# Edge counts built without the staging engine, and four small stages after them joined into one

## The chip, the cores and the metric

The kernel runs on one core of one Trainium2 chip. The metric is the time of one execution on the device, in microseconds (us), lower is better. The kernel before took 2728.32 us (median of 3 runs, 2724.99 to 2728.71).

## The reference, cut to what matters

A graph network of four layers over 2500 nodes with 256 features and 80000 edges. Each layer adds a message-passing part and a routed feed-forward part to x:

```python
edge_index = stack([src, dst])                       # dst is sorted; low numbers are the most frequent
x = x + L0_gnn(_layernorm(x), edge_index, ...)       # mean of x[src] over the edges of each dst, two linear maps
x = x + L0_ffn(_layernorm(x), ...)                   # experts
x = x + L1_gnn(...); x = x + L1_ffn(...)             # normalised by degree, then experts
x = x + L2_gnn(...); x = x + L2_ffn(...)
x = x + L3_gnn(...); x = x + L3_ffn(...)             # attention over edges, then experts
```

Every message-passing part needs only how often each pair (src, dst) occurs, and the degrees (how many edges end at a node). The kernel therefore first turns the edge list into a dense matrix of counts, and uses it four times.

## The kernel before

The program is a row of phases, each with its own block of per-engine instruction streams. At a phase's end all engines meet at a barrier. The change touches the first five: `phase_setup`, `phase_counts`, `phase_degrees`, `phase_transpose_weights` and the first `phase_norm` ("n0"). The sixth is the first gather ("g0"), where the message passing of layer 0 starts. Its first instruction is ScalarE's `g_y` at L847.

**Setup** (L90 to L236) loads the edges as 125 groups of 640, computes two numbers for each edge on VectorE (DVE), `lo` (src modulo 128) and `key` (which encodes dst and src's tile), turns them with TensorE (PE) so that a column holds 128 edges (625 columns in all), and copies them to `lo_col` and `key_col`. Then it finds, for each strip of 16 dst nodes, the first and last column that has an edge of it (`m.ranges`, 160 strips), and the number of units (`m.units`), where a unit is 4 columns.

**Counts** (L239 to L447). There are 20 tiles of 8 strips. For a strip, each unit of 4 columns goes through a ring of SR = 4 slots:

- GpSimd (POOL) loads the tile's 16 bounds into registers (L266), and for each unit writes the unit's 8 edge columns, less the strip's offset, into `key_stage` (L284).
- DVE, in one flat loop over all units (L300), waits for `staged` and `slot_free`, and builds two one-hot matrices: `hot_lo` (4 x 128 wide) and `hot_key` (4 x 320 wide), both from L295.
- PE loads the 16 bounds itself once for each tile (L266), and for each strip opens a PSUM bank with a matmul of zeros (L317), loops over the units with 4 matmuls each (L319, L324), closes with a two-column matmul that tells `summed` (L329), and then takes away the high part of the strip before (L335, `rest`). In strips 2 to 6 of a tile it also turns a fifth of the tile before (L345, 8 matmuls for high and low).
- ScalarE (ACT) copies high (L376) and low (L381) of each strip, and of each fifth the turned high rows (L389) and low rows (L390), each with a sum into `deg_part`.
- SyncE (SP) stores four pieces of 640 KB for each tile (L432, L434, L437, L439). At the end it waits for all of them before the phase may end.

**Degrees** (L580 to L638): DVE sums `deg_part`, takes roots and reciprocals, and the inverse root degrees are spread to a row by 5 f32 matmuls (L637) and 5 copies of ACT.

**Weights and spare row** (L641 to L739): three weight matrices are loaded and turned on PE (L703), and nodes with a degree over 2048 get a spare row: flags, a running sum, `spare_pick` (f32, 128 x 2560, L730), 20 f32 matmuls (40 passes in the profile, L709), an indirect load by POOL (L687), a multiplication (L739), and a store (L672).

**Norm n0** (L504 to L574): DVE takes the statistics of 20 tiles of x, a root on ACT, the normalised tiles (L518), and PE turns them (40 transposes, L574) with 10 copies of ACT (L560).

## Time and profile before

| what | us |
|---|---|
| median of 3 runs | 2728.32 |
| the profiled execution's own time | 2723.45 |
| its span in the trace | 2721.7 |
| setup, until the counts' barrier | 0 to 36.7 |
| counts, until PE's last strip is summed | 36.7 to 409.5 |
| last rows and stores | 409.5 to 425.4 |
| degrees, weights and spare row | 425.4 to 461.6 |
| norm n0 | 461.6 to 480.3 |
| everything from g0 on | 480.3 to 2721.7 |

Times in the trace are from the start of the span. The lines of the source are given as L and a number. "q" behind an engine means its sequencer, which computes registers, branches and waits while the engine's datapath may be busy or idle. "idle before <-X" says for how long the engine stood and who released it; "issue" means that the profile shows nobody that it waited for.

### The profile page before, as it was taken

What the parts mean: (1) busy time and instruction counts of PE and PEld (TensorE: products, weight loads), DVE (VectorE), ACT (ScalarE), POOL (GpSimd) and SP (SyncE); (2) the same over time, 40 slices, a digit from 0 to 9 for tenths busy, and PEclk for the clock granted to TensorE, in tenths of its full rate; (3) what the DMA queues carried; (4) which work ended last, traced back from release to release, by engine and by line L of the source; (5) the groups of instructions that cost most, each with busy time, mean ns of one, the idle gap of its engine ahead of it and who ended that gap; (6) DMA issues with size and microseconds to landing.
All of it is one profiled execution on the core that took longest, in us unless ns stands there. A gap on an engine that the chain in (4) does not pass through costs nothing. (4 is left out here: it accounts for less than half of the span.)

```text
span 2721.7 us, 43328 instructions
## 1 busy us (share of the span) xinstructions
PE 2017.2 (74%) x12867; PEld 1606.2 (59%) x12868; DVE 1540.7 (57%) x2761; ACT 1134.4 (42%) x2295; POOL 512.8 (19%) x581
## 2 busy tenths in 40 slices
PE   3778884893592953882979559934899995699998
PEld 1445553453591532881349449932888885488887
DVE  7877664216347035665124555556899996355554
ACT  0347882101443012782034337712434431276765
POOL 3332320000401001671000057713000000010110
PEclk8999996995795986896989759966999997599999
DMA  1123442410102302563510135521222220000001
GB/s 47 59 116 154 193 193 84 157 39 1 32 1 79 121 5 91 162 184 104 192 33 1 61 127 173 166 92 57 66 84 84 93 86 12 14 13 23 12 24 38
DMA packets 133356, 222.53 MB, mean 82 GB/s; under 512 B 17565, under 2 KB 98973, under 8 KB 133075
## 3 DMA queue, kind: packets, MB, share of 16 engines
q1 hardware_dynamic: 122119, 190.51, 20.7%
q0 software_dynamic: 11088, 30.03, 3.7%
q8 instruction: 93, 1.52, 0.2%
q14 instruction: 56, 0.46, 0.1%
HBM read 146.27 MB, written 74.24 MB: 81 GB/s over the span
## 5 line engine op out<-in xcount | busy, mean ns | idle before, releaser
L807 PE MATMUL g_ps<-g_at,g_y 128*128 128x512 f16 x1170 | 261.8, 386 | 122.1 <-DMA g_at<-counts_t_high 116.5
L1927 DVE TENSOR_TENSOR e_h_low<-x_feat,e_h_high 128x512 fp32r<-128x512 f32 (+1 forms) x240 | 169.6, 709 | 244.7 <-ACT e_h_high L1852 244.7
L2213 DVE SCALAR_TENSOR_TENSOR att_masked<-dinv_row,att_thr,x_feat 128x512 fp32r<-128x512 f32 x400 | 277.2, 747 | 31.4 <-PE att_ps L2324 23.3
L807 PEld LDWEIGHTS g_ps<-g_at,g_y 128*128 128x128 f16 x1170 | 115.6, 99 | 265.5 <-DMA g_at<-counts_t_high 117.1
L1851 ACT ACTIVATE x_feat<-e_hps,e_b 128x512 f32<-128x512 f32 (+1 forms) x240 | 177.7, 740 | 202.0 <-issue 99.4
L2324 PE MATMUL att_ps<-att_xl_parts,att_masked 128*128 128x260 f32 x1600 | 229.9, 294 | 25.7 <-DVE att_masked L2213 23.4
L2324 PEld LDWEIGHTS att_ps<-att_xl_parts,att_masked 128*128 128x128 f32 x1600 | 203.0, 189 | 51.5 <-DVE att_masked L2213 40.4
L324 PE MATMUL count_ps<-hot_key,hot_lo 128*128 x960 | 195.8, 325 | 35.2 <-DVE hot_key L295 23.5
L295 DVE TENSOR_TENSOR hot_key<-o_tok,key_stage 128x1280 f16 x240 | 196.8, 820 | 0.0
L1794 PE MATMUL e_yps<-e_w_high,e_h_high 128*128 128x256 f32 (+1 forms) x640 | 182.2, 285 | 2.2 <-DVE e_h_low L1927 2.2
L1794 PE MATMUL e_yps<-e_w_high,e_h_low 128*128 128x256 f32 (+1 forms) x640 | 180.9, 283 | 0.0
L1794 PE MATMUL e_yps<-e_w_low,e_h_high 128*128 128x256 f32 (+1 forms) x640 | 180.9, 283 | 0.0
L1852 ACT ACTIVATE e_h_high<-e_hps,e_b 128x512 fp32r<-128x512 f32 (+1 forms) x240 | 176.5, 735 | 0.0
L284 POOL TENSOR_TENSOR key_stage<-dinv_row,o_tok x240 | 121.9, 508 | 268.0 <-issue 176.8
L1766 PE MATMUL e_hps<-e_x_high,e_w_high 128*128 128x512 f32 (+1 forms) x320 | 126.5, 395 | 60.0 <-POOL e_w_low L1720 45.9
L324 PEld LDWEIGHTS count_ps<-hot_key,hot_lo 128*128 x960 | 95.7, 100 | 120.1 <-issue 70.9
L1720 POOL TENSOR_TENSOR e_w_low<-a3xn_tok,e_w_high 128x512 fp32r<-128x512 f32 x23 | 30.1, 1336 | 710.2 <-ACT e_w_high L1858 710.2
L295 DVE TENSOR_TENSOR hot_lo<-o_tok,key_stage 128x512 f16 x240 | 102.1, 425 | 92.9 <-PE count_ps L324 61.8
L1457 POOL DMA_INDIRECT e_x_rows<-xn_rows,e_get_i x104 | 129.0, 1241 | 59.2 <-issue 29.9
L376 ACT ACTIVATE turn_high<-count_ps 128x320 f16<-128x320 f32 x160 | 74.8, 468 | 147.8 <-PE count_ps L329 147.7
L2324 PE MATMUL att_ps<-att_xl_parts,att_plain 128*128 128x260 f32 x800 | 107.8, 294 | 32.5 <-ACT att_plain L2293 32.5
L2293 ACT ACTIVATE att_plain<-x_feat 128x512 fp32r<-128x512 f16 x200 | 107.4, 620 | 49.0 <-PE att_ps L2324 42.5
(466 smaller groups left out, 4981.8 us busy)
## 6 DMA issues: line engine op xcount, KB each, us to landing
g_at<-counts_t_high SPq DMA_DIRECT2D x12, 2560.0 KB
x_feat<-counts_high SPq DMA_DIRECT2D x40, 640.0 KB, 4.1
e_w_in<-in_L_ffn_W SPq DMA_DIRECT2D x35, 512.0 KB, 4.0
e_w_in<-in_L_ffn_expert_w SPq DMA_DIRECT2D x56, 256.0 KB, 3.8
counts_t_high<-turn_high SPq DMA_DIRECT2D x20, 640.0 KB, 3.4
counts_t_low<-turn_low SPq DMA_DIRECT2D x20, 640.0 KB, 4.8
counts_high<-row_high SPq DMA_DIRECT2D x20, 640.0 KB, 3.0
counts_low<-row_low SPq DMA_DIRECT2D x20, 640.0 KB, 4.2
```

Of the source, the lines that this page charges most:

```text
L284: pool.tensor_tensor(stage[:, ds(slot_of(n), 1), :, :, :].rearrange("p a i u d -> p (a i) u d"), edge_col[:, :, ds(c, UN)].unsqueeze(3).to ...
L295: return dve.tensor_tensor(out.rearrange("p a u (w d) -> p (a u) w d", d=2), numbers.rearrange("p (w d) -> p w d", d=2).unsqueeze(1).to_br ...
L324: mm = pe.matmul(acc[:, q % 4, 0:KW], hot_lo[:, ds(at, 1), j, :].rearrange("p a l -> p (a l)"), hot_key[:, ds(at, 1), j, :].rearrange("p a ...
L807: pe.matmul(ps[:, k, :], y2[:, part, s, k * P:(k + 1) * P], at[:, b % 2, :, s, :], start=(s == 0 and part == 0), stop=False, skip_group_ch ...
L1457: pool.indirect_dma_start(x_rows[:, b % XB, q, :], None, m.xn_rows[:, :], bass.IndirectOffsetOnAxis(ap=r.get_i[:, b * RT + q:b * RT + q + ...
L1766: mm = pe.matmul(h_ps[0][:, f, 0:width(b)], w_parts[0][w][:, u, k, f * P:(f + 1) * P], x_parts[x][:, k, b * BLK:b * BLK + width(b)], start ...
L1794: mm = pe.matmul(y_ps[0:tokens, q, 0:D], h_parts[-1][h][:, v % 2, k, q * P:q * P + tokens], w_parts[-1][w][:, u, k, :], start=(k == 0 and ...
L1851: act.activation(h_sb[i][:, f, 0:w], h_ps[i][:, f, 0:w], func, bias=bias, scale=scale)
L1852: act.activation(h_parts[i][0][:, v % 2, f, 0:w], h_ps[i][:, f, 0:w], func, bias=bias, scale=scale).then_inc(h_act[i], 1)
L1927: dve.tensor_tensor(h_parts[i][1][:, v % 2, f, 0:w], h_sb[i][:, f, 0:w], h_parts[i][0][:, v % 2, f, 0:w].bitcast(F32), ALU.subtract).then_ ...
L2213: dve.scalar_tensor_tensor(S[:, n % RING, :], EL[:, it % 2, u - 1, :], thr[:, t, h:h + 1], A[:, t, :], ALU.is_gt, ALU.mult).then_inc(maske ...
L2324: mm = pe.matmul(ps[:, n % 2 * TB + q, 0:PW], side[:, q * P:(q + 1) * P], moving, start=(t == 0), stop=(t == NT - 1))
```

## The change

Three functions become part of others, and two are rewritten.

- **Setup.** The two numbers of an edge now carry its strip: `lo` = 128 x (strip within a lot of 32) + lane - 2048, and `key` = 320 x lot + 16 x tile + place - 2048. They are stored as f16, each twice, in `m.edge_col`, by two copies of ACT. The column ranges come from dst alone, ahead of the two numbers. Units are kept for each strip (`m.strip_units`), and their sum is gone. ACT runs one Sqrt at the start.
- **Counts.** POOL has no part. DVE loops over lots, strips and units with register bounds (32 registers loaded for each 16 strips), compares the edge columns directly with a slice of `m.numbers` that depends on the strip and the lot, and computes slot and count in registers. The ring has SR = 8 slots. PE loads 32 unit counts for each 4 tiles. The closing two-column matmul and its semaphore are gone (but for the very first strip): ACT's copy of a strip now waits for `rest` of the strip before it. The two row copies become one of 128 x 1024 with one sum.
- **Norm n0's first part** (statistics, root, normalised tiles) stands behind the last one-hots in the counts phase. ACT takes the root after the last `copy_low`, ahead of the last five row copies.
- **One stage, `prepare`**, does degrees, weights, spare row and the turning of x. The wait for all stores moves into its SP stream; only POOL's indirect load waits for that. `spare_pick` and its matmuls are f16.

```diff
-SR = 4
+SR = 8
+GT = 4
+LOT = 32
...
-            with pool.Fori(0, NT) as t:
-                bounds(pool, t, regs)
...
-            with dve.Fori(0, units) as n:
-                at = slot_of(n)
-                column = stage[:, ds(at, 1), :, :, :].rearrange("p a i u d -> p (a i) u d")
-                dve.wait_ge(staged, n + 1)
-                dve.wait_ge(slot_free, n + 1)
-                one_hot(hot_lo[:, ds(at, 1), :, :], lo_no, P, column[:, 0, :, :])
-                one_hot(hot_key[:, ds(at, 1), :, :], m.src_no[:, 0:KW], KW, column[:, 1, :, :]).then_inc(built, 1)
+            def next_unit(eng, need, at, inside):
+                eng.reg_add(at, at, KW)
+                eng.reg_alu(inside, at, (SR - 1) * KW, ALU.is_le)
+                eng.reg_alu(at, at, inside, ALU.mult)
+                eng.reg_add(need, need, 1)
...
+                with dve.Fori(0, NS // LOT) as h:
+                    first_key = dve.snap(h * KW, min_val=0, max_val=NS // LOT * KW - KW)
+                    for i in range(LOT // (2 * QS)):
+                        dve.reg_load(regs, m.ranges[0:1, ds(h * (LOT // (2 * QS)) + i, 1), :].rearrange("a t n -> a (t n)"))
+                        for q in range(2 * QS):
+                            lanes = (i * 2 * QS + q) * P
+                            dve.reg_mov(column, regs[q])
+                            with dve.Fori(regs[q], regs[2 * QS + q], UN):
+                                dve.wait_ge(slot_free, need)
+                                c = dve.snap(column, min_val=0, max_val=NCOL)
+                                slot = dve.snap(at, min_val=0, max_val=(SR - 1) * KW)
+                                one_hot(hot_lo[:, :, ds(slot, P)], m.numbers[:, lanes:lanes + P], P, m.edge_col[:, 0, ds(c, UN), :])
+                                one_hot(hot_key[:, :, ds(slot, KW)], m.numbers[:, ds(first_key, KW)], KW,
+                                        m.edge_col[:, 1, ds(c, UN), :]).then_inc(built, 1)
+                                dve.reg_add(column, column, UN)
+                                next_unit(dve, need, at, inside)
...
+                    with pe.Fori(0, regs[i * QS + q]):
+                        pe.wait_ge(built, need)
+                        slot = pe.snap(at, min_val=0, max_val=(SR - 1) * KW)
+                        for j in range(UN):
+                            mm = pe.matmul(acc[:, q % 4, 0:KW], hot_lo[:, j, ds(slot, P)], hot_key[:, j, ds(slot, KW)],
+                                           start=False, stop=False, skip_group_check=True)
+                        mm.then_inc(slot_free, 1)
+                        next_unit(pe, need, at, inside)
-                pe.matmul(acc[:, q % 4, 0:2], m.zeros16[:, :], m.src_no[:, 0:2], start=False, stop=False,
-                          skip_group_check=True).then_inc(summed, 1)
...
+                def group(g, first):
+                    pe.reg_load(regs, m.strip_units[0:1, ds(g * (GT * QS), GT * QS)])
+                    for i in range(GT):
+                        tile(g * GT + i, i % 2, i, not first or i > 0)
...
-                act.activation(row_high[:, u, cut], tps[:, (u + b) % 2, 0, :], ACT.Copy, accum_out=m.deg_part[:, ds(t, 1), b])
-                act.activation(row_low[:, u, cut], tps[:, (u + b) % 2, 1, :], ACT.Copy,
-                               accum_out=m.deg_part[:, ds(t, 1), NB4 + b]).then_inc(row_out, 1)
+                    act.activation(row[:, u, :, cut], tps[:, (u + b) % 2, :, :], ACT.Copy,
+                                   accum_out=m.deg_part[:, ds(t, 1), b]).then_inc(row_out, 1)
...
+                for t in range(NT):
+                    own.step(dve.bn_stats(x_st[:, t, :], m.x[:, t, :]))
+                dve.wait_ge(x_own, NT)
+                stats_steps(own, dve, x_st, mean, var, tmp, False)
+                dve.sem_inc(want_root, 1)
+                dve.wait_ge(root, 1)
+                own.join(dve.reciprocal(tmp, var))
+                for t in range(NT):
+                    dve.tensor_scalar(m.xn[:, t, :], m.x[:, t, :], x_stat[:, 0, t:t + 1], x_stat[:, 2, t:t + 1], ALU.subtract, ALU.mult)
...
-            for u in range(2):
-                sp.wait_ge(high_stored[u], NT // 2 * 16)
-                sp.wait_ge(low_stored[u], NT // 2 * 16)
-                sp.wait_ge(row_stored[u], NT // 2 * 32)
+        prepare(nc, m, mats, all_stored)
```

In `prepare` the streams are in this order. PE: 4 of the 10 blocks of turned x, the two flag matmuls, the other 6 blocks, the turned maximum, the 20 pick matmuls, the 12 weight transposes, the 5 spreading matmuls. DVE: degrees, flags, the running sum, `pick`, the reciprocals, the index of the spare row, the 20 diagonal blocks, the maximum, and the product of the fetched row. ACT: block 0 of x, the root, blocks 1 to 9, the 3 weights, the 5 spread rows. SP: the three weight loads, the wait for all stores (which releases POOL's indirect load), and the spare row's store.

## Rows read from the trace of the kernel before

**Rows 1.** Windows of the stages: busy us (instructions) of each engine, granted clock, DMA share, GB/s

```profile
36.70:409.50 372.80, 294.95 (x2198) 175.51 (x2198) 276.33 (x480) 224.68 (x693) 121.91 (x240) 0.93 0.33 130
461.60:480.30 18.70, 7.25 (x40) 7.01 (x40) 14.54 (x49) 5.83 (x11) 0.00 (x0) 0.59 0.00 0
480.30:2721.70 2241.40, 1688.97 (x10496) 1404.95 (x10496) 1211.33 (x2134) 890.37 (x1556) 381.47 (x312) 0.86 0.23 74
```

**Rows 2.** Waits of PE in the counts: total us, times, longest

```profile
PE count_ps L317 <- issue: 36.3, 18, 5.4
PE count_ps L324 <- DVE hot_key L295: 23.5, 50, 2.8
```

**Rows 3.** Register loads by source line: ns min/median/max, first and last start

```profile
L266 PEldq TENSOR_LOAD <-ranges x20: 1103/1107/3205, 37.0 to 396.4; - x20
L292 DVEq TENSOR_LOAD <-units x1: 553/553/553, 36.9 to 36.9; - x1
```

**Rows 4.** One of DVE's unit loops, time order: start, busy, engine, line

```profile
43.44 0.43 DVE L295 TENSOR_TENSOR hot_lo<-o_tok,key_stage 128x512 f16 x1
43.80 0.81 DVE L295 TENSOR_TENSOR hot_key<-o_tok,key_stage 128x1280 f16 x1
44.53 0.43 DVE L295 TENSOR_TENSOR hot_lo<-o_tok,key_stage 128x512 f16 x1
```

**Rows 5.** Sequencer instructions by source line (DVE's loop, SP's three register adds)

```profile
L300 DVEq COMPARE_BRANCH  x240: 50/56/75, 40.4 to 404.1; - x120
L295 DVEq FUSED_REGOPS  x480: 93/93/110, 39.9 to 403.9; - x160
L441 SPq FUSED_REGOPS  x20: 60/100/147, 117.1 to 420.8; - x20
```

**Rows 6.** PE in time order, dense strips, then two late strips

```profile
51.22 0.80 PE L324 MATMUL count_ps<-hot_key,hot_lo 128*128 x4 [0.41 <-DVE hot_key L295]
52.44 0.77 PE L324 MATMUL count_ps<-hot_key,hot_lo 128*128 x4 [0.41 <-DVE hot_key L295]
...
358.36 0.17 PE L329 MATMUL count_ps<-o_tok,zeros 128*128 128x2 f16 x1
...
359.64 0.17 PE L329 MATMUL count_ps<-o_tok,zeros 128*128 128x2 f16 x1
```

**Rows 7.** Window of one late tile

```profile
357.19:370.73 13.54, 11.15 (x96) 7.13 (x97) 9.31 (x16) 11.84 (x39) 4.06 (x8) 1.00 0.48 194
```

**Rows 8.** ACT, one row pair in time order, then a copy of 1024 by source line

```profile
206.60 0.60 ACT L389 ACTIVATE row_high<-cturn_ps 128x512 f16<-128x512 f32 x1
...
207.19 0.59 ACT L390 ACTIVATE row_low<-cturn_ps 128x512 f16<-128x512 f32 x1
...
L854 ACT ACTIVATE g_self<-x_feat x1: 1040/1040/1040, 485.1 to 485.1; 128x1024 f32<-128x1024 f32 x1
```

**Rows 9.** Setup on DVE, its end, and the first one-hot, time order

```profile
10.24 0.49 DVE L163 TENSOR_SCALAR edge_b<-edge_i 125x640 int32<-125x640 int32 x1 [9.15 <-DMA edge_i<-in_dst]
...
15.75 0.82 DVE L176 TENSOR_REDUCE key_ends<-edge_f 125x5 f32<-125x640 f32 x1
...
20.55 0.79 DVE L188 COPY bounds_row<-turn_ps 80x625 f32<-80x625 f32 x1
...
35.66 0.14 DVE L217 CAST units<-ends_row 1x1 int32<-1x1 f32 x1
...
40.09 0.43 DVE L295 TENSOR_TENSOR hot_lo<-o_tok,key_stage 128x512 f16 x1 [4.29 <-POOL key_stage L284]
```

**Rows 10.** From the last strip to g0, time order

```profile
409.47 0.17 PE L329 MATMUL count_ps<-o_tok,zeros 128*128 128x2 f16 x1
...
425.48 0.36 DVE L598 TENSOR_REDUCE deg<-deg_part 128x20 f32<-128x200 f32 x1 [20.47 <-PEq L2451]
...
446.03 5.43 PE L709 MATMUL spare_ps<-spare_rows,spare_pick 128*128 128x2 f32 x40
...
456.97 0.89 DVE L739 TENSOR_SCALAR spare_low<-spare_low,spare_at 128x2560 f16<-128x2560 f16 x1 [5.13 <-DMA spare_low<-counts_low,spare_at_i]
...
461.60 6.63 DVE L504 BATCH_NORM_STATS2 n_st<-x_tok 128x6 f32<-128x256 f32 x20 [3.74 <-PEq L2451]
...
480.31 1.06 ACT L847 ACTIVATE g_y<-xn_tok 128x1024 f16<-128x1024 f32 x1 [0.78 <-PEq L2451]
```

More of the change, by code:

```diff
@@ L173, in _ @@
-            own.join(dve.scalar_tensor_tensor(t_dst, key, -float(NT - 1), t_dst, ALU.mult, ALU.add))
-            own.join(dve.scalar_tensor_tensor(key, t_src, float(WD) / P, t_dst, ALU.mult, ALU.add))
-            by_column = key.rearrange("p (k e) -> p k e", k=GC)
+            dst_f, key_f = edge_t[0:NG, 0, :], edge_t[0:NG, 1, :]
+            lot, lane, tile, place, group = (edge_b[0:NG, i, :] for i in range(5))
+            own.join(dve.tensor_copy(dst_f, dst_i))
+            by_column = dst_f.rearrange("p (k e) -> p k e", k=GC)
@@ L182, in _ @@
-            for i, col in enumerate((m.lo_col, m.key_col)):
-                own.step(dve.tensor_copy(col[:, 0:NCOL].rearrange("p (g k) -> p k g", k=GC),
-                                         ps[:, 2 * i:2 * i + 2, :, :].rearrange("p b q n -> p (b q) n")[:, 0:GC, 0:NG]))
+            own.step(dve.tensor_scalar(lot, dst_i, (LOT - 1) * WD, (P // WD).bit_length() - 1, ALU.bitwise_and, ALU.logical_shift_left))
+            own.step(dve.tensor_scalar(lane, src_i, P - 1, None, ALU.bitwise_and))
+            own.step(dve.tensor_scalar(tile, src_i, (P // WD).bit_length() - 1, -WD, ALU.logical_shift_right, ALU.bitwise_and))
@@ new lines, in _ @@
+            own.step(dve.tensor_scalar(place, dst_i, WD - 1, None, ALU.bitwise_and))
+            own.join(dve.tensor_scalar(group, dst_i, (LOT * WD).bit_length() - 1, None, ALU.logical_shift_right))
+            own.step(dve.scalar_tensor_tensor(edge_f[0:NG, 0, :], lot, float(LOW), lane, ALU.add, ALU.add))
+            own.join(dve.scalar_tensor_tensor(key_f, group, float(KW), tile, ALU.mult, ALU.add))
+            own.step(dve.scalar_tensor_tensor(edge_f[0:NG, 1, :], place, float(LOW), key_f, ALU.add, ALU.add))
@@ L213, in _ @@
             own.join(dve.tensor_copy(span_i[0:1, :], span))
-            own.join(dve.tensor_scalar(span_i[0:1, :], span_i[0:1, :], UN.bit_length() - 1, None, ALU.arith_shift_right))
-            own.join(dve.tensor_copy(span, span_i[0:1, :]))
-            own.join(dve.tensor_reduce(ends_row[0:1, 1, 0:1], span, AX.X, ALU.add))
-            own.join(dve.tensor_copy(m.units[0:1, :], ends_row[0:1, 1, 0:1]))
+            own.join(dve.tensor_scalar(m.strip_units[0:1, :], span_i[0:1, :], UN.bit_length() - 1, None, ALU.arith_shift_right))
+        @block.scalar
+        def _(act):
+            act.wait_ge(made, 1)
+            act.activation(m.spare_col[:, 0:1], m.ones[:, 0:1], ACT.Sqrt)
+            act.wait_ge(turned, 2 * GC)
+            for i in range(2):
+                act.activation(m.edge_col[:, i, 0:NCOL, :].rearrange("p (g k) d -> p k g d", k=GC),
+                               ps[:, 2 * i:2 * i + 2, :, :].rearrange("p b q n -> p (b q) n")[:, 0:GC, 0:NG].unsqueeze(3)
+                               .to_broadcast([P, GC, NG, 2]), ACT.Copy)
         @block.tensor
@@ L221, in _ @@
             pe.wait_ge(made, 3)
-            pe.wait_ge(dve_own, 10)
+            pe.wait_ge(dve_own, 4)
+            for i in range(2):
+                for k in range(GC):
+                    pe.transpose(ps[0:NH, 4 + 2 * i + k // 4, k % 4, 0:NG], bounds[0:NG, i, k, :],
+                                 m.ident[0:NG, 0:NG]).then_inc(turned_rng, 1)
+            pe.wait_ge(dve_own, 12)
             for i in range(2):
```

689 lines of the change are left out of this document (335 added, 354 removed).

## The prediction

> **What bounds the kernel now.** I read the windows by stage first. What the change touches ends at 480.3 us; the 2241.4 us behind it [rows 1] run the same instructions on the same data, so I carry them over unchanged. The counts are the long stage, 372.8 us, and no engine is full in it: PE 294.95, DVE 276.33, ACT 224.68, POOL 121.91 [rows 1]. Next the order in time. DVE alone would make a unit in 1.09 us (43.44 to 44.53) [rows 4], PE takes 1.22 us for each further unit of a strip (51.22 to 52.44, of which 0.41 us stands between the matmuls) and 1.28 us for a late strip of one unit (358.36 to 359.64) [rows 6]. 240 units at 1.09 are 262 us, so DVE has slack, and PE with its sequencer sets the pace. Third the waits: PE stands 36.3 us ahead of L317, at 18 tile starts [rows 2], and these are the register loads of 16 bounds, 20 of them, 1.1 us each and up to 3.2 [rows 3]. A late tile takes 13.54 us, of which ACT is busy 11.84 [rows 7]: ACT is right behind PE. After the last strip (409.47) the phases stand in a row, each behind a barrier, until g0 starts at 480.31: 70.8 us [rows 10], with short dependent instructions that leave every engine mostly idle.
>
> **Part 1, setup.** The range work starts at 20.55 us, behind seven elementwise steps on each edge's two numbers, and setup ends at 35.8 [rows 9]. Now a cast (0.49, as its neighbour there), two reductions (0.82 each) and a copy (0.6) come first, from 10.24 to 13.0; then five integer steps, 0.4 apart, to 15.0, and three of two tensors at 0.8, to 17.4 in place of 20.55. The three last steps (the sum of the units) save 0.85. So setup ends 4.0 us earlier. From setup's end to the first one-hot it is 4.3 us now (35.8 to 40.09), through POOL's load and staging [rows 9]. DVE will instead load 32 registers itself: 1 took 0.55, 16 take 1.11 [rows 3], so 0.037 each, 32 take 1.7; with barrier and loop entry 3.5 us. Saved 4.8 in all; bounds 3 and 6. The two copies and the extra table load on ACT are over before the ranges are, 15 us of cover.
>
> **Part 2, counts.** Four terms.
> (a) Loads. PE's 19 loads inside the stage become 4, of 32 registers. Low end 1.7 (above), high end 3.2 + 16 x 0.037 = 3.8. I take 2.8, which makes 11 us in place of 36.3: -25. The other load is DVE's, 10 of them; 8 slots at 1.3 us are 10 us of cover, so nothing, and at most 9 x 1.7 = 15 if DVE has no lead.
> (b) ACT. The second copy of a row pair starts 0.59 us behind the first (206.60 to 207.19), so a pair takes 1.18; a copy lasts 0.01 longer than that step, and one of 1024 lasts 1.04, so it takes 1.03. That is 0.15 off five times a tile, so ACT falls from 11.84 to 11.1 a tile [rows 7, 8]. With its mean load wait of 1.1 gone a late tile would fall to 12.4; ACT at 11.1 is late next, and in the strips with row copies (about 0.7 for high and low, plus 1.03, against PE's 1.28) it sets the pace until the strips without let it catch up. I give back 0.25 us for each of 12 late tiles: +3.
> (c) Register work. The new loops add up to five register operations for each unit on PE and on DVE, and take away PE's and DVE's mask and add. One fused instruction did three adds on SP in 0.06 to 0.10 us [rows 5]. PE's sequencer is exposed between matmuls in 80 further units and 60 strips without turning: 140 x 0.05 = +7. Bounds: 0 and 240 x 0.15 = 36.
> (d) The closing matmul goes, 0.03 us apart from its neighbour: nothing. That ACT's copy now waits for `rest` costs nothing where ACT is late anyway, and at most 0.1 x 160 = 16 where not; it is inside (c)'s upper bound. POOL's staging goes; it released DVE but rarely, so nothing.
> Sum of part 2: -25 + 3 + 7 = -15. DVE must keep up: 240 units in about 350 us is 1.46 us a unit, against 1.09 now. Its loop holds six sequencer instructions, among them two fused ones of 0.093 and the branch of 0.056 [rows 5]. I put the new unit at 1.2 to 1.3.
>
> **Part 3, the tail.** From the last strip to g0 is 70.8 us now. New, from the last strip X:
> - rest, high, low as before: X + 3, then the root, and five row copies at 1.1 to 1.3 as PE's turnings feed them: X + 10. DVE is some units ahead of PE, so statistics (6.63, and 1.3 of small steps) are done by then, and the 20 normalised tiles (6.55 for all now, by the same instruction) end at X + 10 to X + 13. With the barrier `prepare` starts at X + 12.5. The landing of the last stores, now 5 us ahead of 425.48 [rows 10], is only waited for by the indirect load.
> - In `prepare`, T after its start: 16 transposes of x (7.25 us for 40 [rows 1], so 2.9), flags and matmuls 3.7; running sum 6.3; `pick` as f16, twice the 0.82 of a one-hot of 1280, 7.9. PE finishes the 40 transposes at 8.3, the maximum, then 20 pick matmuls: now 40 passes in 5.43 [rows 10], as f16 half the passes, 2.0 to 2.7, so 10.9. Index at 11.2, indirect load 5.1 as now: 16.3. PE meanwhile turns the weights (3.0, as now) to 13.9, and spreads the row in about 5.6: 19.5. DVE's last diagonal block waits for the fourth of those: 18.5, then the maximum and the product (0.89): 19.9. From there to the next phase is 3.74 us after 457.86 now, by the store's landing: 23.6.
> So g0 starts at X + 36.1 in place of X + 70.8: -34.7. The four pieces that go from the path: the statistics and the normalising (9.9 under the counts' tail), the turning of x (under the flags and the sum), one barrier and a store's landing, and the f32 pick. Bounds: -25 (the spreading, the indirect load and the store each 3 us late) and -40 (the indirect load hidden, DVE's work ended by X + 10).
>
> One rule of the Trainium skill speaks against part 2. The trace shows 16 registers in 1.11 us as the median of PE's 20 loads, and 3.2 at most [rows 3]. "Runtime: NRT & Kernel Launch", section "Instruction fetch mechanics", puts a TENSOR_LOAD at about 200 ns for each register even in bulk. By that rule 32 registers take 6.4 us, and PE's four loads would cost 26 and not 11 us: the sum would be 15 us higher. The median load here contradicts it, the slowest fits it.
>
> **Sum.** -4.8 - 15 - 34.7 = -54.5. The profiled execution took 2723.45 (its span is 2721.7, 1.75 outside), which gives 2669; the median of the runs lies 4.9 above it: 2728.3 - 54.5 = 2673.8. I say 2673. A difference of under 0.2% (5.5 us) can't be told from none here.
>
> **Rivals.**
> - *DVE becomes the pace* (20%). For: up to five register operations, three run-time addresses and a nested loop in its sequencer, which takes part of each 1.09 us now. Against: fused operations are cheap [rows 5]. At 1.5 us a unit the counts take 240 x 1.5 + 17 of loads = 377 against 369.4 (40.09 to 409.47) [rows 9, 10]: +8, with the normalising behind it 3 later: -4.8 + 8 - 32 = -29, 2699.
> - *Slower than before, by the same sequencer* (5%). It decides from (369.4 + 4.8 + 32 - 17) / 240 = 1.62 us a unit. At 1.7 the counts take 425, and the whole is +19: 2747. It would need 0.5 us more of sequencer work for each unit than the loop now has in all its instructions' own durations.
> - *Loads of 32 registers are slow* (10%), 6.4 us each, as if the slow rows were the rule (3.2 for 16): 4 x 6.4 = 26, so part 2 gives nothing and the sum is -39.5: 2689.
> - *All of the loads' time comes back* (15%): PE's loads hide in its queue, register work costs nothing, ACT catches up: part 2 is -30 to -36, and the sum -70 to -75: 2655.
> - *`prepare` is longer* (7%): its spare-row chain stands behind PE's transposes and the spread rows; at 33 us and not 23.6 the tail gives -25: 2683.
> - The forecast itself has 43%.
>
> **How the numbers follow.** The range 2642 to 2702 holds the forecast, the slow loads, the longer stage, most of the full gain, and DVE's pace up to 1.5. Faster by over 0.2% is all but the second rival and a part of the first: 0.93; same 0.02; slower 0.05.
>
> **What would show it.** In the profile after: the first one-hot near 35.3 us; one-hots that start less than 1.3 us apart in the dense strips with PE's 1.2 to 1.3 us between them; register loads of PE at 4 inner places, 1.7 to 3.8 us; a late tile of about 12.4 us with ACT busy 11; the last strip near 390; the gap from it to L847's successor near 36 us. Wrong would be: DVE's one-hots with gaps not ended by PE (its sequencer is the pace); a span from the last strip to g0 over 45 us; or any change behind g0, which I hold at 2241 us.

## The result

The kernel after takes 2627.15 us (median of 4 runs, 2624.22 to 2630.38), beside 2728.45 for the kernel before in the same comparison: a ratio of 0.9632, 95% interval 0.9615 to 0.9649. It is 101 us faster. The forecast was 2673 us, 55 us faster, in a range from 2642 to 2702; the measured time lies 15 us below the range. The direction was right, the size was not.

The profiled execution took 2628.58 us and has a span of 2626.9. First the windows of its stages (window, length, then busy us and instructions of PE, PE's weight loads, DVE, ACT and POOL, granted clock, DMA share, GB/s):

```profile
35.30:350.00 314.70, 264.94 (x2040) 161.43 (x2040) 269.82 (x507) 208.88 (x506) 0.00 (x0) 0.98 0.37 155
348.65:380.46 31.81, 20.19 (x131) 14.00 (x129) 18.16 (x72) 18.56 (x39) 2.20 (x7) 0.77 0.49 179
380.46:2626.90 2246.44, 1691.19 (x10496) 1407.77 (x10496) 1211.54 (x2134) 890.69 (x1556) 381.91 (x312) 0.86 0.23 73
```

Against [rows 1] and [rows 10], with the counts taken from the first one-hot to the start of the last unit's last matmul:

| stretch | before | after | measured | forecast |
|---|---|---|---|---|
| start to the first one-hot | 40.09 | 35.59 | -4.5 | -4.8 |
| counts | 369.2 | 313.0 | -56.2 | -15 |
| tail, from there to g0 | 71.1 | 31.8 | -39.3 | -34.7 |
| g0 to the end | 2241.4 | 2246.4 | +5.0 | 0 |
| sum | 2721.7 | 2626.9 | -94.8 (rounded terms -95.0) | -54.5 |

The stretch behind g0 runs the same instructions; over the seventeen changed kernels here it lies between 2240.1 and 2248.3 us, and the kernel before, at 2241.4, lies inside that spread, so nothing shows the +5.0 to be an effect of the change. Almost the whole miss is in the counts. Their waits (total us, times, longest):

```profile
DVE hot_lo L478 <- PE count_ps L526: 31.4, 33, 4.3
PE count_ps L520 <- issue: 18.9, 5, 5.7
PE count_ps L526 <- DVE hot_key L478: 13.6, 37, 1.2
```

The load waits of PE that [rows 2] has at 18 tile starts, 36.3 us, are now 18.9 us at 5. The loads themselves (count, ns min/median/max, first and last start):

```profile
L563 PEldq TENSOR_LOAD <-strip_units x5: 2331/2566/4297, 32.9 to 300.5; - x5
L486 DVEq TENSOR_LOAD <-ranges x10: 2112/2933/5872, 32.9 to 315.7; - x10
```

Loads give back 17 to 18 us of the 56 (PE's waits fall by 17.4, its loads from 32.3 us in all to 14.4). DVE's ten loads, which I had put at nothing, took 31.7 us in all, but PE's waits for `hot_key` did not grow: 13.6 us in all, against 23.5 [rows 2].

PE's granted clock moved too, and I had not priced that. Over the counts it is 0.94 before and 0.98 after. At the lower of its two levels (1.2 GHz) two matmuls of a unit start 0.26 us apart, otherwise 0.14 to 0.15; 120 of the 960 unit matmuls ran so before, 43 after. 18 of them stand at the start of the counts in both. The others come in short stretches, eleven before and three after, and each begins 1 to 5 us after the start of a load for which PE stood (before: loads at 90.8, 117.0 and 141.9, lower level from 94.7, 118.6 and 145.9). That is worth at most some 9 us of the 56 (77 x 0.12, an estimate that puts every one of them on the path), and runs 8 and 11 below speak for less.

The rest is in the pace. A dense strip is one with many units, as in the first tiles; a late strip has one. In a dense strip DVE and PE now go in step (start, busy, and in brackets the idle time before it and who ended it); first DVE, then PE:

```profile
50.59 0.41 DVE L478 TENSOR_TENSOR hot_lo<-o_tok,dinv_row 128x512 f16 x1
50.93 0.81 DVE L478 TENSOR_TENSOR hot_key<-o_tok,dinv_row  x1
51.66 0.41 DVE L478 TENSOR_TENSOR hot_lo<-o_tok,dinv_row 128x512 f16 x1
...
52.73 0.41 DVE L478 TENSOR_TENSOR hot_lo<-o_tok,dinv_row 128x512 f16 x1
```

```profile
50.83 0.74 PE L526 MATMUL count_ps<-hot_key,hot_lo 128*128 x4
51.90 0.72 PE L526 MATMUL count_ps<-hot_key,hot_lo 128*128 x4 [0.33 <-DVE hot_key L478]
52.97 0.76 PE L526 MATMUL count_ps<-hot_key,hot_lo 128*128 x4 [0.36 <-DVE hot_key L478]
```

A unit takes 1.07 us on both. Before, PE took 1.22 [rows 6] and DVE could do 1.09 [rows 4]. A late tile went from 13.54 us [rows 7] to 11.40, with ACT busy 10.59, and its row copy of 1024 lets the next copy start 1.00 us later (233.89 to 234.89):

```profile
229.12:240.52 11.40, 10.09 (x89) 6.59 (x89) 9.30 (x17) 10.59 (x28) 0.00 (x0) 1.00 0.56 230
```

```profile
233.89 1.03 ACT L594 ACTIVATE count_row<-cturn_ps 128x1024 f16<-128x1024 f32 x1
234.80 0.21 ACT L594 ACTIVATION_READ_ACCUMULATOR count_row<-cturn_ps  x1
234.89 0.45 ACT L581 ACTIVATE turn_high<-count_ps 128x320 f16<-128x320 f32 x1
```

The tail, in time order, to be read against [rows 10]: PE, then DVE, then ACT's first instruction of g0.

```profile
359.45 3.52 PE L325 MATMUL turned_ps<-ident,xn_tok 128*128 128x128 f32 x16 [2.51 <-PEq L457]
367.56 0.64 PE L348 MATMUL spare_ps<-spare_rows,spare_pick 128*128 128x4 f16 x20 [1.46 <-DVE spare_pick L390]
370.32 6.15 PE L332 MATMUL deg_ps<-deg_diag,ones 128*128 128x512 f32 x10
```

```profile
365.92 1.49 DVE L390 TENSOR_TENSOR spare_pick<-spare_no,spare_col 128x2560 f16<-128x2560 f16 x1
...
375.69 0.89 DVE L412 TENSOR_SCALAR spare_low<-spare_low,spare_at 128x2560 f16<-128x2560 f16 x1
```

```profile
380.46 4.84 ACT L877 ACTIVATE g_y<-xn_tok 128x1024 f16<-128x1024 f32 x5 [3.36 <-PEq L2477]
```

### The profile page after: what moved, and what is told of

Its sections match the earlier page's. It is cut to its first block and busy times, and to the rows that moved or that the text cites. A ratio compares the mean times of both kernels' runs of the same rounds, so it can differ in the third digit from the quotient of the medians.

```text
span 2626.9 us, 39157 instructions
## 1 busy us (share of the span) xinstructions
PE 1981.1 (75%) x12688; PEld 1587.2 (60%) x12689; DVE 1519.6 (58%) x2752; ACT 1120.7 (43%) x2100; POOL 392.4 (15%) x339
## 5 line engine op out<-in xcount | busy, mean ns | idle before, releaser
L2243 DVE SCALAR_TENSOR_TENSOR att_masked<-dinv_row,att_thr,x_feat 128x512 fp32r<-128x512 f32 x400 | 277.2, 747 | 31.8 <-PE att_ps L2354 23.6
L478 DVE TENSOR_TENSOR hot_key<-o_tok,dinv_row x240 | 195.4, 814 | 0.0
L526 PE MATMUL count_ps<-hot_key,hot_lo 128*128 x960 | 177.1, 309 | 18.5 <-DVE hot_key L478 13.6
L2323 ACT ACTIVATE att_plain<-x_feat 128x512 fp32r<-128x512 f16 x200 | 107.5, 620 | 49.3 <-PE att_ps L2354 42.8
L1824 PEld LDWEIGHTS e_yps<-e_w_high,e_h_high 128*128 128x128 f32 (+1 forms) x640 | 121.2, 189 | 8.5 <-issue 3.7
L2354 PEld LDWEIGHTS att_ps<-att_xl_parts,att_plain 128*128 128x128 f32 x800 | 105.2, 193 | 34.6 <-ACT att_plain L2323 34.6
L1796 PE MATMUL e_hps<-e_x_low,e_w_high 128*128 128x512 f32 (+1 forms) x320 | 126.0, 394 | 0.0
```

Of the source, the lines that this page charges most:

```text
L478: return dve.tensor_tensor(out.rearrange("p u (w d) -> p u w d", d=2), numbers.rearrange("p (w d) -> p w d", d=2).unsqueeze(1).to_broadcas ...
L526: mm = pe.matmul(acc[:, q % 4, 0:KW], hot_lo[:, j, ds(slot, P)], hot_key[:, j, ds(slot, KW)], start=False, stop=False, skip_group_check=True)
L1796: mm = pe.matmul(h_ps[0][:, f, 0:width(b)], w_parts[0][w][:, u, k, f * P:(f + 1) * P], x_parts[x][:, k, b * BLK:b * BLK + width(b)], start ...
L1824: mm = pe.matmul(y_ps[0:tokens, q, 0:D], h_parts[-1][h][:, v % 2, k, q * P:q * P + tokens], w_parts[-1][w][:, u, k, :], start=(k == 0 and ...
L2243: dve.scalar_tensor_tensor(S[:, n % RING, :], EL[:, it % 2, u - 1, :], thr[:, t, h:h + 1], A[:, t, :], ALU.is_gt, ALU.mult).then_inc(maske ...
L2323: act.activation(plain[:, n % ARING, :], A[:, t, :], ACT.Copy).then_inc(plain_a, 1)
```

## The experiments

Each kernel is the one after with one edit, unless it says otherwise; the edits are cut to their main lines (`...`). "Measured" gives the median in us, its ratio to the kernel before and the ratio's 95% interval. "Counts" and "tail" are the two stretches of the table, in us, from the profile of that run; after has 313.0 and 31.8. Each comes from one profiled execution. Runs 6 and 14, which leave the counts' loops as they are, have 312.4 and 312.9, and run 7, which only takes DVE's norm out of that phase, 314.3: differences of 1 to 2 us in the counts can't be told from none.

**1. Slot arithmetic on PE.** After, PE keeps byte offset and count in registers, and the four operations of `next_unit` are one fused sequencer instruction of 154 ns. Here PE masks a counter, as before.

```diff
-                        pe.wait_ge(built, need)
-                        slot = pe.snap(at, min_val=0, max_val=(SR - 1) * KW)
+                        n = pe.snap(used)
+                        at = n & (SR - 1)
+                        pe.wait_ge(built, n + 1)
...
-                        next_unit(pe, need, at, inside)
+                        pe.reg_add(used, used, 1)
```

> The changed kernel, with PE's unit loop computing its slot as the kernel before did (a counter, a mask, and a multiplied slot in each matmul's address) and nothing else changed. Theory A (the unit itself became shorter in PE's sequencer, 1.21 to 1.07 us): the pace of PE in strips of two units goes from 2.21 back to about 2.5 us a strip, the counts from the first one-hot to the last sum (313 us) grow by 15 to 30 us. Rival B (the deeper ring freed the engines from each other): no change, under 3 us.

Measured: 2636.59 us, ratio 0.9671 (0.9639 to 0.9704). Counts 325.4, +12.4. The edit undoes PE's half of the term that I had booked at +7, and that half alone is a gain. PE's sequencer, after and with the mask (ns min/median/max):

```profile
L526 PEldq FUSED_REGOPS  x720: 55/55/65, 36.9 to 348.2; - x180
L460 PEldq FUSED_REGOPS  x240: 149/154/168, 37.3 to 348.4; - x120
L524 PEldq FUSED_REGOPS  x240: 59/59/59, 36.8 to 347.8; - x120
```

```profile
L528 PEldq FUSED_REGOPS  x960: 55/55/65, 36.8 to 360.7; - x192
L528 PEldq ALU_OP  x240: 36/36/42, 36.7 to 360.2; - x120
```

After has five fused instructions for a unit beside its branch: three addresses, one that holds the wait and the first address, and the update. With the mask there are seven: four addresses, mask, copy and add. A unit of a dense strip takes 1.09 to 1.14 us in place of 1.07.

**2. Ring of four slots.**

```diff
-SR = 8
+SR = 4
```

> The changed kernel with SR = 4. Theory A: only the register loads lose cover, DVE's ten and PE's four, 0 to 12 us on the counts, and tiles without a load keep their 17.5 and 11.4 us. Rival B (the ring): every tile grows, the counts by 20 us or more.

Measured: 2623.52, 0.9623 (0.959 to 0.9656), counts 312.2. The deeper ring shows no gain.

**3. The closing matmul of a strip.**

```diff
+                    pe.matmul(acc[:, q % 4, 0:2], m.zeros16[:, :], m.numbers[:, 0:2], start=False, stop=False,
+                              skip_group_check=True).then_inc(summed, 1)
...
-                    act.wait_ge(rest_mm, t * QS + (q + 2))
+                    act.wait_ge(rest_mm, t * QS + (q + 1))
```

> The changed kernel with the closing two-column matmul and its semaphore back in each strip; ACT's high copy waits for it again. Theory A: 160 strips at 0.03 to 0.06 us, 5 to 10 us on the counts at most. Rival C (the closing matmul held PE's queue between strips, and its going is most of the 0.43 us by which a strip of two units got shorter): 0.15 us or more for each strip, over 20 us.

Measured: 2628.11, 0.964 (0.9601 to 0.9679), counts 312.4. Nothing, as forecast.

**4. PE's loads, 8 registers for each tile in place of 32 for four.**

```diff
-                    pe.reg_load(regs, m.strip_units[0:1, ds(g * (GT * QS), GT * QS)])
                     for i in range(GT):
+                        pe.reg_load(regs[i * QS:(i + 1) * QS], m.strip_units[0:1, ds(g * (GT * QS) + i * QS, QS)])
```

> The changed kernel with PE loading 8 unit counts at each tile (20 loads) and not 32 for four tiles (5 loads). Theory A (loads cost by the number of them, not of registers): 15 more stalls at 1 to 3 us: the counts grow by 15 to 35 us. Rival D (loads cost by the register, the same 160 registers in all): under 3 us.

Measured: 2620.55, 0.9612 (0.958 to 0.9644). Counts 308.9, 4.1 less than after, although there are four times as many loads:

```profile
L564 PEldq TENSOR_LOAD <-strip_units x20: 588/594/785, 33.2 to 333.8; - x20
```

The cost is by register: 8 take 0.59, 16 take 1.10 [rows 3], 32 take 2.13 in run 8, which is 64 ns for each (0.51 for 8, 1.03 for 16) and some 0.08 fixed. What the change gained is that it loads one count for a strip, not a first and a last column: 160 registers and not 320. Grouping them by four tiles gained nothing; its loads were 14.4 us in all, these 12.1. A late tile with a load of 8 takes 11.64 us here, one without a load took 11.38 after, and one with a load of 32 took 14.48: much of a short load is hidden, little of a long one. The granted clock, too, stays at its full level from 40.0 us on (up to there no clock is recorded, and the ten slow matmuls of this run stand there):

```profile
35.91:344.80 308.89, 264.22 (x2037) 159.04 (x2038) 269.71 (x507) 207.13 (x504) 0.00 (x0) 1.00 0.38 158
```

**5. Two row copies again.**

```diff
-                    act.activation(row[:, u, :, cut], tps[:, (u + b) % 2, :, :], ACT.Copy,
-                                   accum_out=m.deg_part[:, ds(t, 1), b]).then_inc(row_out, 1)
+                    act.activation(row[:, u, 0, cut], tps[:, (u + b) % 2, 0, :], ACT.Copy, accum_out=m.deg_part[:, ds(t, 1), b])
+                    act.activation(row[:, u, 1, cut], tps[:, (u + b) % 2, 1, :], ACT.Copy,
+                                   accum_out=m.deg_part[:, ds(t, 1), NB4 + b]).then_inc(row_out, 1)
```

> The changed kernel with ACT's row copy split in two again, 512 wide each, each with its own sum. If ACT is what sets the late tiles (11.38 us, steps of 1.66 where rows are copied): each of the five steps goes to 1.81, a late tile to about 12.0, the counts grow by 8 to 12 us. If PE's or DVE's sequencer sets them: under 2 us.

Measured: 2631.35, 0.9648 (0.962 to 0.9676). Counts 322.1, +9.1. The late tile is 0.75 us longer, which is five times the 0.15 that the prediction had for a pair: ACT is the pace there, and every saved tenth on it counts.

```profile
231.38:243.53 12.15, 10.12 (x89) 6.61 (x89) 9.24 (x17) 11.35 (x38) 0.00 (x0) 1.00 0.54 216
```

The two copies and the next one on ACT: from 231.25 to 232.39 it is 1.14 us, where one copy of 1024 takes 1.00.

```profile
231.25 0.74 ACT L594 ACTIVATE count_row<-cturn_ps 128x512 f16<-128x512 f32 x1
231.82 0.75 ACT L595 ACTIVATE count_row<-cturn_ps 128x512 f16<-128x512 f32 x1
232.39 0.60 ACT L581 ACTIVATE turn_high<-count_ps 128x320 f16<-128x320 f32 x1
```

**6. All stores waited for at the end of the counts.** Three waits of SP stand there again.

```diff
+                for u in range(2):
+                    sp.wait_ge(high_stored[u], NT // 2 * 16)
+                    sp.wait_ge(low_stored[u], NT // 2 * 16)
+                    sp.wait_ge(row_stored[u], NT // 2 * 32)
```

> The changed kernel with the wait for all stores back at the end of the counts' own block. If the landing of the last stores was on the path: the stretch from the last sum to g0's first instruction (31.6 us) grows by 3 to 5 us. If DVE's normalised tiles end later than the landing anyway: under 1 us.

Measured: 2626.94, 0.9632 (0.9604 to 0.966). In the profile the tail is 35.0, +3.2. The median of the times does not show it, and its interval is too wide to show or exclude 3 us.

**7. The norm behind the counts.** Statistics, root and normalised tiles stand in a block of their own ahead of `prepare`.

```diff
+        with nc.Block() as block:
+            @block.vector
+            def _(dve):
+                own = Steps(dve, x_own)
...
+            @block.scalar
+            def _(act):
+                act.wait_ge(want_root, 1)
+                act.activation(x_stat[:, 1, :], x_stat[:, 1, :], ACT.Sqrt).then_inc(root, 1)
```

> The changed kernel with statistics, root and normalised tiles in a block of their own between the counts and the joined stage. If what was hidden under the end of the counts is what the tail gained: the stretch from the last sum to g0 grows by about 15 us (6.6 + 1.3 + 6.6 + a barrier of 0.8), less the 2 to 4 us by which the counts' block ends earlier without it: 11 to 14. If the joined stage waits for something else: under 5.

Measured: 2641.56, 0.9686 (0.9655 to 0.9716). Tail 47.7, +15.9: the two passes over x, 6.63 and 6.54 us, with the small steps and a barrier, are bare again.

```profile
361.26 6.63 DVE L644 BATCH_NORM_STATS2 x_st<-x_tok 128x6 f32<-128x256 f32 x20 [20.93 <-PEq L457]
...
369.57 6.54 DVE L651 TENSOR_SCALAR xn_tok<-x_tok,x_stat 128x256 f32<-128x256 f32 x20
```

**8. Turnings apart from each other.** If ACT sets the pace in strips with a row copy, they should not stand in a row.

```diff
-TURNS = (2, 3, 4, 5, 6)
+TURNS = (1, 2, 4, 5, 7)
```

> The changed kernel with the five turnings of a tile in strips 1, 2, 4, 5 and 7 in place of 2 to 6. If ACT's row of five 1.66 us steps sets a late tile (11.38 us) while PE and DVE could do with 10: the tile falls to about 10.6, the counts by 8 to 12 us. If the pace of PE's sequencer is the floor: under 2 us.

Measured: 2615.22, 0.9589 (0.9559 to 0.962), counts 304.3, 8.7 less than after. The late tile is 10.96 us with ACT busy 10.71; and PE's loads no longer begin beside the issue of a store, 2.13 to 2.33 us in place of 2.33 to 4.30, which is 3.5 us less in all. The rows are the late tile, then the loads:

```profile
225.05:236.01 10.96, 9.59 (x92) 6.62 (x89) 9.02 (x17) 10.71 (x27) 0.00 (x0) 1.00 0.58 239
```

```profile
L563 PEldq TENSOR_LOAD <-strip_units x5: 2129/2145/2328, 32.9 to 294.1; - x5
```

**9. POOL stages the keys again**, one operation and one semaphore ahead of DVE.

```diff
+                            pool.wait_ge(built, n + 1)
+                            pool.tensor_tensor(stage[:, ds(n & (SR - 1), 1), :, :, :].rearrange("p a i u d -> p (a i) u d"),
+                                               m.edge_col[:, :, ds(c, UN), :], none, ALU.add).then_inc(staged, 1)
...
+                                dve.wait_ge(staged, need)
                                 dve.wait_ge(slot_free, need)
```

> The changed kernel with POOL staging each unit's columns again (a copy, since the strip stays inside the pairs) and DVE reading the stage and waiting for it. If the staging was part of the pace: POOL starts a unit 0.6 us after the ring lets it and loads 32 registers for each 2 tiles at 3 us, so the counts grow by 10 to 20 us, mostly in tiles after a load. If POOL's stage was always ahead (my forecast held it for nothing): the counts grow by under 3 us, and the first one-hot comes 1 us later.

Measured: 2638.05, 0.9674 (0.9653 to 0.9696). First one-hot at 36.35, +0.8, and counts 322.0, +9.0. Tile 0, all dense strips, takes 49.82 in place of 45.49; late tiles are unchanged (11.36). So the cost is in the dense strips: tile 0 and, by 0.2 to 2.4 us each, tiles 1 to 4 have nearly all of it. The edit does not isolate POOL, for DVE's loop gets a second wait, a counter and a mask with it.

**10. Five parts together, then with staging.** Ring of 4, PE's mask, closing matmul, two row copies, and 16 registers loaded for each tile (eight of them are used); the second kernel adds POOL's staging.

```diff
+                        at16 = g * (GT * QS) + (i * QS if first and i == 0 else i * QS - QS)
+                        pe.reg_load(regs[0:2 * QS], m.strip_units[0:1, ds(at16, 2 * QS)])
```

> The changed kernel with ring of 4, PE's slot as before, the closing matmul, two row copies, and PE loading 16 registers at each of 20 tiles as before. Alone the slot gave +12.4 us on the counts, the rows +9.1, ring and closing matmul -0.8 and -0.6. Sum with 16 registers a tile (before: 32.3 us of loads in all against 14.4): about 313 + 20 + 14 = 347. If 347 or less is reached, some 22 us of the 56 are still unnamed (POOL's staging); if 365 to 369, these parts are all of it.

Measured: 2664.7, 0.9772 (0.975 to 0.9794), counts 351.5, +38.5. PE's 20 loads are again of 16 registers, 29.0 us in all (32.3 before):

```profile
L566 PEldq TENSOR_LOAD <-strip_units x20: 1102/1108/2694, 32.7 to 374.1; - x20
```

> The same with POOL's staging as well. If the list is complete: counts of 365 to 370 us, as before the change (369.2), and late tiles of 13.5. If under 355: something else in the change (the strip inside the pairs and DVE's own loop) is worth the rest.

Measured: 2675.13, 0.981 (0.9788 to 0.9833), counts 355.8, +42.8. 13.4 us of the 56.2 were left unexplained.

**11. Loads of 8 and the turnings apart, together.** The edits of 4 and 8.

> The changed kernel with PE loading 8 unit counts at each tile and the turnings in strips 1, 2, 4, 5 and 7. The two alone gave -4.1 and -8.7 us on the counts. If they are independent: 300 us of counts, 2614 us. If the loads only filled gaps that the turnings left: 304.

Measured: 2615.87 (2615.18 to 2617.49), 0.9593 (0.9579 to 0.9607). Counts 305.6. They do not add: with the turnings apart the loads of 32 are already short (10.9 us in all, these 12.1). 16 unit matmuls are slow here, all at the start, where run 8 has 47, and yet the counts are no shorter than in run 8: the clock's share of the time is small.

**12. The layout of the ring.** After, a slot is a stretch of columns inside each of a unit's four rows, so one offset serves both one-hot tiles. Here the slot's index is outermost, as before, and both engines mask a counter.

```diff
-            nc.sbuf_tensor("hot_lo", [P, UN, SR * KW], F16) as hot_lo,
-            nc.sbuf_tensor("hot_key", [P, UN, SR * KW], F16) as hot_key,
+            nc.sbuf_tensor("hot_lo", [P, SR, UN, P], F16) as hot_lo,
+            nc.sbuf_tensor("hot_key", [P, SR, UN, KW], F16) as hot_key,
```

> The one-hot tiles with the ring's index outermost, as before, and the slot worked out of a counter on DVE and PE, as before; all else as after. If the 13.4 us that four_parts_and_stage leaves over are PE's address instructions: these take 74 ns again in place of 55, four for a unit, PE needs 1.21 us between the units of a dense strip in place of 1.07, and the counts last about 25 to 30 us longer than after (313.0), 12 to 18 more than in pe_slot_as_before (325.4): some 2652 us in all. If the layout is nothing and the rest comes from the loop of units on DVE (one loop over all units before, loops inside strips after): as pe_slot_as_before, 2636 us and 55 ns.

Measured: 2647.52, 0.9717 (0.9702 to 0.9732). Counts 337.7, which is 12.3 more than in run 1. First PE's sequencer at the line of the unit's matmuls, then PE in a dense strip:

```profile
L528 PEldq FUSED_REGOPS  x960: 74/74/88, 37.4 to 373.7; - x192
```

```profile
50.83 0.80 PE L528 MATMUL count_ps<-hot_key,hot_lo 128*128 x4 [0.41 <-issue]
52.04 0.76 PE L528 MATMUL count_ps<-hot_key,hot_lo 128*128 x4 [0.41 <-issue]
```

74 ns for an address, and 1.21 us from unit to unit. The 0.41 us stands there as "issue". [Rows 6] have the same 0.41 with DVE's name on it: it was PE's own sequencer then too. In time order the kernel before has the same list there: add (L328), branch (208 ns), copy (L320), mask and address (L324), each some 60 ns behind the one ahead of it, with no wait between them:

```profile
L320 PEldq FUSED_REGOPS  x240: 41/41/46, 38.5 to 408.3; - x120
L324 PEldq FUSED_REGOPS  x960: 74/74/88, 41.4 to 409.0; - x192
L324 PEldq ALU_OP  x240: 36/36/42, 41.3 to 408.4; - x120
L328 PEldq FUSED_REGOPS  x240: 42/42/42, 42.1 to 409.2; - x120
```

**13. All parts back.** `four_parts_and_stage` with that layout.

> four_parts_and_stage with the old slot layout on top: ring of 4, closing matmul, two row copies, 16 registers loaded for each tile, POOL staging the keys, slot from a counter, ring index outermost. Setup, tail and DVE's loops inside the strips stay as after. If nothing else made the counts long: 369 us from the first one-hot to the last sum, as before (369.2), and some 2689 us. If the strips' loops on DVE are worth something by themselves: less, near 356 to 360, and 2675 to 2680 us.

Measured: 2678.16, 0.9826 (0.9811 to 0.9841). Counts 365.5, against 369.2 before: the difference of 56.2 is undone but for 3.7. The second and the third tile have that remainder (3.8 us, of which 1.1 are shorter load stalls); no late tile differs by more than 0.6. The clock came back as well: 111 unit matmuls at the lower level, against 120 before and 43 after.

**14. The pick in 32 bits.**

```diff
-        nc.sbuf_tensor("spare_pick", [P, NT, P], F16) as pick,
+        nc.sbuf_tensor("spare_pick", [P, NT, P], F32) as pick,
```

> After, with the pick of spare rows in 32-bit floats (numbers, rows and pick), as before. If the 16-bit pick is what made the tail shorter than forecast (pick matmuls 0.64 us where 2.0 to 2.7 were reckoned, the pick itself 1.49 us): the tail, 31.8 us, becomes 35 to 37 and the time 2630 to 2632 us. If other work hides it: 2627 us.

Measured: 2633.29, 0.9667 (0.9652 to 0.9681). The tail is 40.1, +8.3, more than either side had:

```profile
369.02 6.92 PE L348 MATMUL spare_ps<-spare_rows,spare_pick 128*128 128x4 f32 x40 [2.41 <-DVE spare_pick L390]
```

```profile
366.05 2.82 DVE L390 TENSOR_TENSOR spare_pick<-spare_no,spare_col 128x2560 f32<-128x2560 f32 x1
```

6.92 us here and 0.64 us after for the same 20 products. The larger number is not the format's doing alone, because the granted clock fell to its lower level in the middle of these passes:

```profile
369.00:370.90 1.90, 1.88 (x17) 1.90 (x18) 0.51 (x4) 0.00 (x0) 0.00 (x0) 1.00 0.00 0
371.40:376.00 4.60, 4.60 (x23) 4.60 (x23) 0.00 (x0) 0.00 (x0) 0.00 (x0) 0.50 0.00 0
```

A pass starts every 0.112 us in the first window and every 0.214 in the second, where 22 passes cost some 2.2 us more than at the full level. Before, 31 of the 39 steps took 0.112 or less, which is why it took 5.43 [rows 10]. In 16 bits a pass starts every 0.025 us, at clock 1.00. So like for like the 20 products take some 4.5 us in 32 bits (40 x 0.112) and 0.5 in 16 bits, and of the +8.3 of the tail some 2 us are the clock.

**15. One instruction less on paper.** `turns_spread` with slots 512 columns apart in a ring of 4, so that the offset needs an add and a mask, not an add, a compare and a multiply.

```diff
-                eng.reg_add(at, at, KW)
-                eng.reg_alu(inside, at, (SR - 1) * KW, ALU.is_le)
-                eng.reg_alu(at, at, inside, ALU.mult)
+                eng.reg_add(at, at, STEP)
+                eng.reg_alu(at, at, SR * STEP - 1, ALU.bitwise_and)
                 eng.reg_add(need, need, 1)
```

> turns_spread with the ring's offset kept by one add and one mask in place of an add, a compare and a multiply (ring of 4, slots 512 columns apart), so that DVE and PE have one sequencer instruction less for a unit. DVE is the pace of the dense strips at 1.07 us per unit, of which some 0.15 us is not its two one-hots: if the sequencer's instructions stand in that gap, a unit takes about 0.04 to 0.05 us less and the counts 4 to 8 us less than in turns_spread (304.3), some 2609 us. If they run ahead of DVE: 2615 us as turns_spread.

Measured: 2629.22, 0.9647 (0.9634 to 0.9661): slower than `turns_spread` by 14 us, counts 319.2 against 304.3 (the ring of 4 was nothing in run 2). The update of PE's registers is no longer one instruction:

```profile
L461 PEldq ALU_OP  x240: 32/32/42, 37.5 to 354.9; - x120
L462 PEldq ALU_OP  x240: 36/36/36, 37.6 to 355.0; - x120
L463 PEldq FUSED_REGOPS  x240: 42/42/42, 37.7 to 355.1; - x120
```

```profile
52.90 0.71 PE L526 MATMUL count_ps<-hot_key,hot_lo 128*128 x4 [0.42 <-issue]
53.99 0.75 PE L526 MATMUL count_ps<-hot_key,hot_lo 128*128 x4 [0.38 <-issue]
```

Add, compare, multiply and add go as one instruction of 154 ns. Add, mask and add go as three, each with some 60 ns behind it, and PE is back at 1.09 to 1.14 us for a unit.

## Why the prediction was wrong

The step that failed is part 2 (c). The prediction priced the new register work as time added to PE's (+7 us, at least zero); in the runs that work is shorter than the old, and undoing it costs 22 us of counts (12.4 and 9.7). Next comes (b), which was booked as +3 and is a gain of 9.1. The forecast's mechanism for the sum was a gain of the loads with something given back. The counts in fact gained in five places. The reversals account for them:

| undone, on top of the rows above | counts | step |
|---|---|---|
| nothing (after) | 313.0 | |
| slot arithmetic on PE | 325.4 | 12.4 |
| two row copies | | 9.1 (alone, run 5) |
| with them ring, closing matmul, loads of 16 for each tile | 351.5 | 17.0 (38.5 - 12.4 - 9.1) |
| POOL's staging | 355.8 | 4.3 (9.0 when undone alone) |
| ring layout | 365.5 | 9.7 (12.3 on top of run 1) |
| not found | 369.2 | 3.7 |

The steps depend on the order in which parts are undone, and the 17.0 is what is left when the two terms above it are taken as additive. Against the forecast of -15 the miss of 41.2 is then 29.1 from (c), 12.1 from (b), 4.3 from (d) and 3.7 not found, less 8.0 by which (a) was too high.

- **Part 1, setup: right.** -4.8 forecast, -4.5 measured.
- **Part 2 (a), loads: direction right, for the wrong reason.** 25 us forecast, 17.0 by the runs, a remainder that holds the ring and the closing matmul too, which alone did nothing, and what of the clock comes with the load stalls (PE's loads fell from 32.3 to 14.4 us in all). I worked out 0.037 us for a register from one load of DVE (0.553) and one of PE (1.107) [rows 3], two engines, and so took the number of loads as the cost. It is the number of registers, at 0.064. By the Trainium skill, "Runtime: NRT & Kernel Launch", section "Instruction fetch mechanics", a register takes about 200 ns even in bulk, which by estimate is 6.4 us for 32. Here, where the registers come from a tile in SBUF, no load of PE took that; 8, 16 and 32 registers give 64 ns each, and the measurement decides.
- **Part 2 (b), ACT: the sign was wrong.** The 0.15 us of a pair was nearly right (1.14 for two copies and 1.00 for one, where I had 1.18 and 1.03), and five of them a tile are what run 5 gives back for a late tile. But I booked it only as a smaller ACT floor and then took 3 us off the gain; undone, it costs 9.1. I put a late tile at 12.4 with ACT busy 11; it is 11.4 with ACT busy 10.6.
- **Part 2 (c), register work: the step that failed.** I counted operations in the source and priced them as additions, +7 us, with a lower bound of zero, and so excluded a gain. But the chain between two units of PE, 0.41 us in [rows 6], was all of it sequencer work (run 12); [rows 5] showed DVE's and SP's sequencers, not PE's, and I should have listed PE's chain before and after. It lost two instructions and each address lost 19 ns: undone, 12.4 and 9.7 us, a gain of 22 where I had a loss of 7. (The layout's 9.7 includes the mask in DVE's loop; that PE's addresses are what counts is read from run 12's rows, where PE is the pace.)
- **Part 2 (d), the small ones.** The closing matmul is nothing, as forecast. POOL's staging was not nothing: 4.3 on top of the rest, 9.0 alone (with DVE's extra register work in both), in the dense strips, where DVE is the pace once PE is quicker. "Released DVE but rarely" did not fit the trace before either, which has it 65 times in 240 units (total us, times, longest):

```profile
DVE hot_lo L295 <- POOL key_stage L284: 23.1, 65, 4.3
```

- **Part 3, the tail: right within its bounds.** X + 36.1 forecast, 31.8 measured. The new stage starts at 10.8 and not 12.5, and lasts 21.0 and not 23.6. Of this, pick matmuls of 0.64 us where I had 2.0 to 2.7: I took half the passes as half the time, but each pass is shorter too (0.025 us and not 0.112 at the same clock). The norm under the last strips is worth 15.9 us, the wait for the stores 3.2 in the profile, the 16-bit pick 8.3, of which some 2 are the clock.
- **The rivals.** "DVE becomes the pace" did happen in the dense strips, but at 1.07 us, not at 1.5: it ended a gain and caused no loss. "All of the loads' time comes back", 2655, had the nearest time and the wrong cause. Slow loads of 32 did not occur as priced: 2.3 to 4.3 us, against 6.4.
- **Why the range failed.** Its low end, 2642, came from part 2 at -36 at best; with setup at its bound of -6 and the tail at -40 that sum is -82, 2646. With a bound of zero on (c) and nothing on (d), no case could reach -56 in the counts. The clock stood in no term.

Still open: the last 3.7 us of the counts, which could be DVE's one loop over all units in place of loops for each strip, shorter loads beside the stores, or the spread of single profiles. None was tried by itself. Nor did any run separate the clock from the load stalls that it follows, or POOL's staging from what it adds to DVE's loop.

The runs point to a better version: `TURNS = (1, 2, 4, 5, 7)`, 2615.22 us (median of 2 runs), and with loads of 8 beside it 2615.87 (median of 5, 0.9593 of before), which is 11 to 12 us under after.

## What to carry to other kernels

Where an engine's run-time loop is short, list its sequencer's instructions in time order, before and after, and count instructions, not operations: a series that fuses is cheap, and one operation less that breaks the fusing costs more. Idle time that the profile puts on a releaser is to be checked against that chain, and two durations of PE are compared only at the same granted clock. Never bound a term on the pace-setting engine at zero because the edit "adds" work, and when a bound engine gets quicker, price again every part that had been called hidden.

## What the runs showed of the hardware

- A register load costs by register: 0.59 us for 8, 1.10 for 16, 2.13 for 32 on PE. The same load took 2.97 to 3.21 us for 16 in five tiles before, each begun within about a microsecond of the row stores' issue (stores at 116.2, 140.9, 165.6, load at 117.0, 141.9, 166.2), and up to 5.87 for DVE's 32. That the stores cause it fits the times and run 8, but was not isolated.
- A matmul with run-time addresses on both operands costs 74 ns of PE's sequencer when the two offsets differ and 55 when one register serves both.
- Between two such instructions of PE's sequencer lie some 60 ns in which nothing is recorded, so seven short ones lost to five.
- In f32, 128x128 by two or by four columns, a pass started every 112 ns at granted clock 1.00 and every 214 at 0.50, two passes for a product; in f16 one pass every 25 ns at 1.00.
- ACT's copy of 1024 with a sum lets the next copy start after 1.00 us, two of 512 after 1.14; a late tile with five pairs showed 0.15 of it for each.
- Behind the start of the counts, each stretch at the lower clock began 1 to 5 us after the start of a register load for which PE stood: eleven stretches before, three after, and none in the two kernels with loads of 8.
